# Router logits in four PSUM partition groups, and the first mixer chunks laid among the router's work, in a two-layer recurrent kernel

## What is computed

```python
xn = _layernorm(x)
s = _L0_attn_ref(xn, ...)          # mixer
g = _silu(_L0_ffn_ref(xn, ...))    # router and experts
x = x + s * g
# then layer 1 of the same form, with a selective scan and a binarised matrix

def _L0_attn_ref(x, ...):          # x is xn here
    xn = _rmsnorm(x, rms_w, EPS)
    out_gate = silu(xn @ Wga.T) * (xn @ Wgb.T)
    f = sigmoid(xn @ Wf.T + Wf_b)
    z = (xn @ Wz.T) * sigmoid(xn @ Wzg.T)
    h = _linear_scan(f.astype(bfloat16), z.astype(bfloat16))   # h = f*h + z
    return (out_gate.astype(bfloat16) * h) @ Wout.T + Wout_b + x

def _L0_ffn_ref(x, ...):
    logits = x @ Wr + br           # Wr is 256 x 4
    top_w, top_idx = top_k(softmax(logits), 1)
    return expert[top_idx](x) * top_w
```

## Time and profile before

| | us |
|---|---|
| median of 3 runs | 1426.78 |
| lowest to highest | 1424.15 to 1427.94 |
| profiled execution | 1428.33 |
| its span | 1426.5 |

### The profile page before, as it was taken

One profiled execution on the slowest core, in us unless ns is written; L12 is line 12 of the kernel. 1 busy time (PEld: TensorE's weight loads), 2 busy tenths in 40 slices (PEclk: granted clock), 3 DMA queues, 4 the chain that ended last, 5 costly groups with the idle time before them and its releaser, 6 DMA issues.

```text
span 1426.5 us, 23438 instructions
## 1 busy us (share of the span) xinstructions
PE 1358.4 (95%) x8598; PEld 1075.7 (75%) x8628; DVE 1012.5 (71%) x1358; ACT 880.9 (62%) x1459; POOL 904.1 (63%) x578
## 2 busy tenths in 40 slices
PE   8899999999999999989899999999999999999988
PEld 4444559999999988956677777777777678678777
DVE  7755543322332353488998999999989989989897
ACT  4211121111111133489999989999999999999983
POOL 4222211222222211369999999999999999999995
PEclk9999999999999999999999999999999999999999
DMA  9921126766776756232332533524433523523542
GB/s 298 400 94 59 59 82 234 267 245 247 268 255 245 267 198 222 93 87 75 96 91 67 128 94 88 131 64 119 105 95 91 130 71 91 133 75 94 129 96 68
DMA packets 57762, 205.18 MB, mean 144 GB/s; under 512 B 6575, under 2 KB 32815, under 8 KB 48822
## 3 DMA queue, kind: packets, MB, share of 16 engines
q1 hardware_dynamic: 42358, 146.55, 29.4%
q0 software_dynamic: 15296, 57.19, 17.5%
HBM read 141.78 MB, written 31.00 MB: 121 GB/s over the span
## 4 chain that ended last, share of the span: by engine, by line
PE 60%; POOL 23%; DVE 7%; issue 6%; ACT 2%; DMA 2%; POOLq 0%; DVEq 0%; ACTq 0%
POOL hst L731 18%; PE bank L1654 17%; PE bank L1599 9%; PE bank L1667 8%; PE bank L1821 5%; PE bank L1708 3%; PE bank L1841 3%; DVE hst L1497 2%; PE bank L1738 2%; POOL xpad L674 2%; PE bank L1700 2%; POOL dbuT L695 2%; PE bank L1719 2%; PE bank L1829 2%; PE bank L1629 2%
## 5 line engine op out<-in xcount | busy, mean ns | idle before, releaser
L1497 DVE TENSOR_TENSOR_SCAN hst<-dA,carry,bank 128x512 f32<-128x512 f32 x512 | 631.6, 1269 | 61.8 <-PE bank L1821 39.8
L731 POOL TENSOR_TENSOR hst<-hst,c_bc 128x2048 f32<-128x2048 f32 x127 | 582.3, 4614 | 17.1 <-POOL carry L726 3.0
L938 ACT ACTIVATE dA<-delta,negA 128x512 f32<-128x512 f32 x512 | 354.1, 713 | 9.1 <-DVE hst L1497 8.8
L1821 PEld LDWEIGHTS bank<-ident,dbuT 128*128 128x128 f32 x2048 | 241.6, 141 | 146.5 <-issue 65.6
L1821 PE MATMUL bank<-ident,dbuT 128*128 128x128 f32 x2048 | 310.6, 276 | 33.3 <-DVE hst L1497 29.4
L927 ACT ACTIVATE dbuT<-duT,bT 128x512 f32<-128x512 f32 x382 | 269.3, 712 | 7.0 <-PE bank L1821 7.0
L1654 PEld LDWEIGHTS bank<-f_sb,w_gu 128*128 128x128 f32 x2240 | 256.1, 192 | 5.3 <-issue 2.9
L1654 PE MATMUL bank<-f_sb,w_gu 128*128 128x128 f32 x2240 | 256.9, 275 | 0.7 <-ACT f_sb L795 0.7
L1841 PE MATMUL bank<-ident,hst 128*128 128x128 f32 x1520 | 209.5, 274 | 3.8 <-POOL hst L731 2.9
L659 POOL TENSOR_TENSOR x_sb<-x_sb,neg_half 128x1 f32<-128x1 f32 x35 | 22.7, 648 | 274.5 <-DVE x_sb L1281 274.5
L1841 PEld LDWEIGHTS bank<-ident,hst 128*128 128x128 f32 x1520 | 174.9, 142 | 6.0 <-POOL hst L731 4.1
(11 more groups left out here) (218 smaller groups left out, 1703.9 us busy)
## 6 DMA issues: line engine op xcount, KB each, us to landing
w_gu<-in_w_gu SPq DMA_DIRECT2D x35, 2048.0 KB, 7.4
c_bc<-c_rows SPq DMA_DIRECT2D x64, 512.0 KB, 4.2
hst<-hst POOLq DMA_DIRECT2D x31, 1024.0 KB, 9.1
sorted_x<-sg_a SPq DMA_DIRECT2D x12, 387.0 KB, 12.0
x_sb<-sorted_x SPq DMA_DIRECT2D x35, 129.0 KB, 7.2
x_sb<-in_x SPq DMA_DIRECT2D x8, 512.0 KB, 7.2
w_d<-in_w_d SPq DMA_DIRECT2D x1, 4096.0 KB, 20.3
x_mix<-x_sb SPq DMA_DIRECT2D x1, 4096.0 KB, 30.8
```

The lines of the kernel that those rows point to most:

```text
L731: pool.tensor_tensor(h[:], h[:], c, ALU.mult).then_inc(hc_ready, 1)
L938: act.activation(dA[:, at % DA_BUFS, :], delta[q % B][:, d, :], ACT.Exp, scale=negA[:, d, n:n + 1]).then_inc(dA_ready, 1)
L1497: v.tensor_tensor_scan(h[:, d, :], dA[:, at % DA_BUFS, :], bank[4 + u % 2][:], carry1[q % B][:, n, d:d + 1], ALU.mult, ALU.add).then_inc(s ...
L1821: ins = pe.transpose(bank[4 + u % 2][:, i * P:(i + 1) * P], dbuT[(DS * q + n) % DBU_BUFS][:, i, d * P:(d + 1) * P], ident[:])
```

## The change

The logits are made for two chunks at a time. `w_r` is padded from 4 to 32 columns, and tile i of a chunk writes its logits to PSUM partitions 32*i to 32*i+31, in 16 matmuls of 128 columns in place of 4 of 512. ACT copies one block for two chunks, and one matmul with a strided part of the identity turns four tiles back. Turned inputs share two banks instead of four. F and ZG of chunk 0 stand behind chunks 2 and 3's logits, Z and GA behind those of 4 and 5, GB at the end. The ranks move from chunk 0 into chunk 1. On DVE the first half of chunk 0 stands ahead of the bias splitting and the logits; the router's choice follows add 0; `place_rows` follows chunk 1's second half. `mix_st` becomes `xr_st`; `tri`, `ones`, `empty` and `wo_r` move into the expert weight buffers, so SP also waits for the zero fill and the split ahead of `load_up`.

```diff
             sp.wait_ge(eid_ready, 1)
+            sp.wait_ge(split_ready, 1)
+            sp.wait_ge(zero_filled, 16 * (ROWS // FILL))
             load_up(0)
             load_up(1)
             with sp.Fori(0, CHUNKS - 1) as c:
                 store_mixed(c)
...
-        mix_st = rt[:].rearrange("p k t e -> p (k t e)").rearrange("p (t d) -> p t d", d=D)
+        mix_st = xr_st[:]
...
@@ ScalarE @@
+            for c in range(0, CHUNKS, 2):
+                turn_inputs(c)
+                turn_inputs(c + 1)
+                if c == 2:
+                    scale_w0()
+                copy_logits(c // 2)
+                if c == 2:
+                    forget(0, 0)
+                    gate_z(0, 0)
+            gate_a(0, 0)
+            mixer_half(0, 1)
+            mixer_half(1, 0)
             act.wait_ge(shifted, 1)
             act.activation(rt[:, 2], rt[:, 1], ACT.Exp).then_inc(exp_ready, 1)
...
@@ VectorE @@
+            mixer_half(0, 0, 0)
+            split_biases()
+            take_logits()
+            mixer_half(0, 1, 0)
+            v.wait_ge(xr_turned, KB * CHUNKS)
+            then(rows(0))
+            add_mix(0)
+            choose()
+            mixer_half(1, 0, 0)
+            rank_rows()
+            mixer_half(1, 1, 0)
+            place_rows()
+            tags(0)
+            then(rows(1))
+            add_mix(1)
+            tags(1)
+            mixer_half(2, 0, 0)
+            rows(2)
+            tags(2)
+            mixer_half(2, 1, 0)
+            add_mix(2)
...
@@ TensorE @@
-            def logits(c, u):
-                pe.wait_ge(xrT_ready, KB * c + KB)
-                wait_past(pe, logits_copied, c - 1)
-                for k in range(KB):
-                    at = (c * KB + k) * CH
-                    ins = pe.matmul(bank[4 + u][0:NE, :], w_r[:, k, :], xT[:, at:at + CH], start=(k == 0),
-                                    stop=(k == KB - 1))
+            def logits(p):
+                pe.wait_ge(xrT_ready, KB * (2 * p + 2))
+                wait_past(pe, logits_copied, p)
+                for c in range(2):
+                    for k in range(KB):
+                        for i in range(TPC):
+                            at = ((2 * p + c) * KB + k) * CH + i * P
+                            ins = pe.matmul(bank[6][i * QUAD:(i + 1) * QUAD, c * P:(c + 1) * P], w_r[:, k, :],
+                                            xT[:, at:at + P], start=(k == 0), stop=(k == KB - 1))
                 ins.then_inc(logits_made, 1)
...
+            def turn_logits(c):
+                pe.wait_ge(logits_copied, c // 2 + 1)
+                at = c * TPC * NE
+                pe.matmul(bank[7][:, at:at + TPC * NE].rearrange("p (i e) -> p i e", e=NE), logitsT[:, c % TPC, :],
+                          ident[:].rearrange("p (i e) -> p i e", e=QUAD)[:, :, 0:NE], start=True,
+                          stop=True).then_inc(logits_ready, 1)
...
+            turn_inputs(0)
+            turn_inputs(1)
+            logits(0)
+            turn_inputs(2)
+            turn_inputs(3)
+            logits(1)
             pe.wait_ge(w0_scaled, KB)
             project(0, 0, PROJ_F)
+            project(0, 0, PROJ_ZG)
...
```

More of the change, by code:

```diff
@@ L156 @@
 WARM = 10
-GAP = 152
+GAP = 96
+QUAD = 32
 FIRST_TURN, BANK_A, BANK_B = -2, 6, 7
@@ L768, in _ @@
[L768 to L780, removed]
+                    act.copy(xT[:, at:at + CH], bank[k][:]).then_inc(xrT_ready, 1)
@@ new lines, in rank_rows @@
+            def rank_rows():
+                v.wait_ge(exp_ready, 1)
+                then(v.tensor_reduce(rs[:, 2, :], ex, AX_X, ALU.add))
+                then(v.reciprocal(top_w[:], rs[:, 2, :]))
+                v.wait_ge(ranks_ready, 1)
+                then(v.tensor_copy(tot, bank[0][:, 2 * TILES * NE:3 * TILES * NE]))
+                then(v.memset(rs[:, 3, :], 1.0))
+                for e in range(NE):
+                    then(v.tensor_tensor_scan(cum[:, :, e], rs[:, 3, :], tot[:, :, e], 0.0, ALU.mult, ALU.add))
@@ L1229, in mixer @@
-                assert k[0] == SB * L0_SB == L0_STEPS
-                if early == 0:
-                    rows()
-                    v.wait_ge(st_ready, 1)
+                    return c * L0_STEPS + s * L0_SB + k[0]
+                v.wait_ge(proj_ready, r + PROJ_Z + 1)
+                v.wait_ge(sig_ready, 6 * c + 3 * s + 2)
+                w1 = chain(v.tensor_tensor(z_sb[:, s, :], bank[2 + PROJ_Z][:], sg_z[:, s, :], ALU.mult))
+                v.wait_ge(v_l0, w1)
+                v.wait_ge(carry_set, B)
@@ L1242, in _, with mixer @@
                 v.memset(carry0[b][:], 0.0).then_inc(carry_set, 1)
+            mixer_half(0, 0, 0)
[19 more added lines that the diff above has]
+            add_mix(2)
+            assert [STORED[k] % B for k in range(3)] == [0, 0, 0] and 3 < A_CHUNKS
+            def mixer(c, b):
+                rows(c)
+                tags(c)
+                mixer_half(c, 0, b)
+                mixer_half(c, 1, b)
+                add_mix(c)
             for of_a in (True, False):
                 for b in range(B):
[L1245 to L1250 removed]
+                    run = [k for k in range(3, CHUNKS) if (STORED[k] < A_CHUNKS) == of_a and STORED[k] % B == b]
+                    if len(run) == 1:
+                        mixer(run[0], b)
+                    elif run:
+                        with v.Fori(run[0], run[-1] + 1) as c:
                             mixer(c, b)
```

245 lines of the change are left out of this document (117 added, 128 removed).

## The result

| | before | changed |
|---|---|---|
| median us (4 runs each, same chip) | 1427.28 | 1439.24 |
| lowest to highest | 1424.15 to 1427.94 | 1437.28 to 1440.31 |
| profiled execution, us | 1428.33 | 1440.31 |
| its span, mean granted clock | 1426.5, 0.996 | 1438.5, 0.989 |

The changed kernel takes 1.0086 times as long (95% interval 1.0074 to 1.0097). The prediction was 1437.8 us; in terms of the profiled execution, 1439.3 against 1440.31.

What follows compares the result with a forecast made beforehand. PE alone was taken to bound the kernel from 67.09 us on. Front -6.3, long idle +15.2, second wait +1.9 and hand-over 0.2 gave +11.0 us: 1439.3 profiled, 1437.8 median, range 1430 to 1444.

Steps and rivals of the forecast that it cites:

- L: PE's time for the logits of two chunks in the front, 3.6 us before, taken as 1.5 us.
- No side by side: Rival: the logits' partition groups do not overlap on PE, L = 3.6, time 1443 us; chance 0.08.
- The walk: Step-by-step times of the front, ending with chunk 1's output at 81.0 us against 87.31, a gain of 6.3 us.
- A colder front: Rival: the clock falls between 14 and 25 us, up to 2 us more, 1440; counted within the forecast case's 0.66.
- The long idle: PE's wait ahead of GB of chunk 2 for chunk 1's adds behind `place_rows`, put at 15.2 us.
- E: The time `eid` is ready, at the end of `place_rows`, put at 84.6 us, 26 us later than before.
- (a): From E on SP: two 2 MB loads are issued by E+3.7, only then the store of chunk 0.
- (b): From E on POOL: chunk 0's last scatter is issued at E+5.3 and lands 7.4 us later, at E+12.8.
- (c): From E on DVE: rows 1 to E+14.2, store landed at E+15.2, both adds done at E+16.7.
- Short wait: Rival: weights alone don't slow chunk 0's scatters and store; adds end at E+10.8, time 1432 us; chance 0.15.
- The second wait: PE's wait ahead of chunk 2's output for `gated`, held up by scatters and rows 2, put at 1.9 us.
- Faster: Rival: same waits, but E so early that they fall where PE was still ahead; 1418 us with quick landings; chance 0.07.

Runs made afterwards that it cites:

- e6: The changed kernel with 18 extra matmuls, their results unread, put where PE paused in the front; 1440.69 us, ratio 1.0092.
- e4: The changed kernel with the edits of e2 and e3, and chunk 2's rows and tags behind its second half; 1427.96 us, ratio 1.0007.
- e3: The changed kernel with rows, tags and places of its own for chunk 1, so rows 1 wait for no scatter; 1441.38 us, ratio 1.0097.
- e2: The changed kernel with chunk 0's store alone moved ahead of the expert weight loads; 1438.94 us, ratio 1.0095.
- e7: The changed kernel with e3's own staging for chunk 1 and e1's order of loads and stores; 1425.05 us, ratio 0.9993.
- e1: The changed kernel with the two expert weight loads issued behind the stores of chunks 0 to 3; 1434.68 us, ratio 1.005.
- e8: e7 with e6's 18 matmuls and the bias split ahead of chunk 0's first half on DVE; 1422.02 us, ratio 0.9964.
- e10: e7 with the 18 unused matmuls, the bias split left where the change has it; 1423.52 us, ratio 0.998.
- e9: e8 without its 18 unused matmuls, the bias split still ahead of chunk 0's first half; 1423.97 us, ratio 0.9986.
- e5: The kernel before with only the logits made in four partition groups, order of everything else unchanged; 1425.37 us, ratio 0.9993.

## Why the prediction was right, and where its terms were off

1. **Logits (L = 1.5, bounds 0.9 and 3.6): right in kind, the gain put too low.** The 32 passes take 1.01 us from their start at 35.48 to the turning back at 36.49, 0.032 us a pass. One behind the other each was 0.112, or 0.12 in e6's matmuls of the same shape. So the rival *No side by side* is out. Chunks turn back at some 0.25 us each (predicted 0.2).
The Trainium skill (TensorEngine Tiling (Array Packing), Theoretical Speedup) states up to 4x; the trace has 3.6/1.01 = 3.6, nearer to that rule than my 1.5 was.

2. **The front's gain: predicted 6.3 us, measured 3.5.** The term that is missing from the sum is the clock. The walk had F and ZG from 24.9 to 28.4; they ran from 26.48 to 32.43. I had the cause as a rival (*A colder front*, up to 2 us), not in the sum, and e6 sizes it for this execution: 3.2 us at chunk 1's output (83.77 against 80.60), where e4's and e3's profiles of the same front would give 0.8 and 4.2. With the clock held the walk ends within half a microsecond, in part since errors cancel: in e6 F starts 0.7 us later than in the walk, the logits are 0.5 us a pair shorter, GB of chunk 0 starts at 42.95 (walk: 43.1) and chunk 1's output ends at 80.60 (walk: 81.0). The bias split delays `gated` as forecast, and the wait for it was 1.51 us (predicted 1.6). The two table loads of Exp came and were hidden, on ACT:

```profile
68.91 1.28 ACT L801 ACT_TABLE_LOAD   x1
...
70.53 1.28 ACT L772 ACT_TABLE_LOAD   x1
```

3. **The long idle: predicted 15.2 us, measured 16.51.** E came at 87.47 (predicted 84.6, late by the front's 2.8). The chains (a), (b) and (c) are there, with E + 15.1 for the last scatter (I took the 7.4 us of before, it was 9.8) and E + 16.5 for the store (predicted E + 15.2). That E + 15.2 is 0.7 us more than its own terms: counted from the loads' issue at E + 1.6, 11.5 us for the bytes and 1.4 for the store make E + 14.5. By these terms the idle would have been 14.5 us and the sum 0.7 us further from the result, so a little of the agreement is luck. e2 and e3 show that both chains hold the adds, e4 and e7, with both gone, that nothing else holds them for more than 1.4 us. The rival *Short wait* is out: in e2 the store had been issued long before, at 63.38 us, and with the weights alone in flight the scatters took 7.9 to 9.5 us, against 2.5 to 3.0 without the weights (e1). The Trainium skill (DMA: Bandwidth & Descriptors, Queues, rings and completion order) states that a DMA engine serves its queues in turn, a packet at a time; the trace agrees in so far as the first three scatters, which come from POOL's queue, land by 100.5 us, ahead of the second load, which was issued before two of them and lands at 102.6. That the turns go by packets no run here shows.

4. **The second wait: predicted 1.9 us of idle on PE, measured none.** The rows of chunk 2 did wait for the scatter (3.27 us, 113.74), and `gated` came late. But PE was later still: its 28 passes took 14.31 us instead of e4's 12.28, because of the low clock left by the idle. I had counted that cost as hidden inside the wait; it was the other way round, and it comes to the same: from the adds to chunk 2's output 17.4 us, predicted 17.2.

5. **The sum: predicted +11.0 at chunk 2's output, measured +15.3; and +12.0 at the end.** Here the argument failed at one sentence: from there on both kernels have the same order, so I measured the change at that one point. The order is the same, the clock isn't. 3.3 us came back behind the mixer, 2.8 of them in layer 1, and in part cancelled the 4.3 us by which the sum was short (2.8 by the front, 1.3 by the idle, 0.2 at the end). That the profiled execution ends within 1.0 us of its forecast is to that extent luck.

6. **Faster** was to need `eid` by 74.2 us (by the sum's own 118.5 - 84.6 = 33.9 us, 73.6). No experiment brought it there: in e8, the fastest, `eid` is ready at 82.7 us. Those that became faster (e8 to e10) did so by taking the coupling away and by a front shorter by a few microseconds.

## What to carry to other kernels

When a step is moved, follow every DMA that it releases and every buffer it hands on: here a block of 7 us moved behind the mixer's second chunk brought 4 MB of weights, a store and a scatter into the one place where single staging buffers left PE no slack, and cost over 16 us. Two waits of equal length side by side look like one in the profile; taking either away alone shows nothing, so try both before dropping the idea. On a kernel that PE bounds, a gain of one to three microseconds can be given back by a stretch at 1.2 GHz elsewhere: look at the granted clock over the whole span before believing or dismissing it. And compare two variants by a stage's rows only where the clock is the same in both, as e8 and e10 are in the front and e7 and e9 are not.

## What the runs showed of the hardware that I had not expected

- Float32 matmuls of 32 output partitions in four groups do run side by side, at 0.032 us for 128 columns, against 0.12 us in one group (e6). Their weight loads, one per pass, last 110 to 124 ns each and overlap as well: in the changed kernel 128 of them fill only 3.8 us.
- Eighteen matmuls that compute nothing of use, about 4.6 us of PE's time laid in its pauses, went with a clock of 2.4 GHz through the whole front in all three kernels that have them (e6, e8, e10); in all eight profiles with the logits in four groups and without them it fell to 0.50 there for 3.4 to 13.7 us. Against the same kernel without them, chunk 1 came forward by 2.9 to 4.3 us.
- An idle of 1.43 us (e7) left the clock at 1.00, an idle of 16.51 us brought it to 0.50 and it stayed there for some 4 us of work behind it: 14.31 us for what takes 12.28. In between the length of the pause alone doesn't decide: behind a pause of 2.41 us (e4) the clock fell to 0.50 some 1.2 us into the work, behind 3.57 us it was at 0.50, behind 3.41 us at the same place (e5) it stayed at 1.00.
- 2 MB loads landed in 8.0 and 13.0 us, a 0.5 MB store behind them in 13.6 us and behind nothing in 2.9.
